# Two transformer layers on one core: features laid out so that one DMA carries a part, fp32 queries and projections in layer one, and scalings of two numbers written one number at a time

## The reference

```python
x = x + tanh(g_xattn[0]) * attention0(layernorm(x), ctx)            # w_q, w_k, w_v, w_o, no bias
x = x + tanh(g_ffn[0])   * ternary_ffn(layernorm(x))                # 256 -> 1024 -> 256, weights rounded to -1, 0, 1
x = x + tanh(g_xattn[1]) * attention1(layernorm(x), ctx, distances) # scores - log(distance) * |scale|
x = x + tanh(g_ffn[1])   * expert_ffn(layernorm(x))                 # relu, expert 0 alone, then a layernorm

def _quant_act(x):   # both inputs of the ternary FFN's matmuls
    scale = 127.0 / clip(max(abs(x), axis=-1), EPS)
    return clip(round(x * scale), -128, 127) / scale
```

## Time and profile before

| | |
|---|---|
| median of 3 runs | 430.17 us (428.62 to 430.37) |
| profiled execution | 433.62 us, span of the trace 431.9 us |
| PE busy | 333.7 us, 77% |
| DVE busy | 309.8 us, 72% |
| ACT busy | 282.7 us, 65% |
| POOL busy | 233.1 us, 54% |
| granted TensorE clock, mean | 0.920 |

### The profile page before, as it was taken

One profiled execution on the slowest core, in us unless ns is written; L12 is line 12 of the kernel. 1 busy time (PEld: TensorE's weight loads), 2 busy tenths in 40 slices (PEclk: granted clock), 3 DMA queues, 4 the chain that ended last, 5 costly groups with the idle time before them and its releaser, 6 DMA issues.

```text
span 431.9 us, 9332 instructions
## 1 busy us (share of the span) xinstructions
PE 333.7 (77%) x3346; PEld 269.8 (62%) x3346; DVE 309.8 (72%) x663; ACT 282.7 (65%) x515; POOL 233.1 (54%) x414
## 2 busy tenths in 40 slices
...
GB/s 237 278 93 180 27 62 77 29 30 30 39 40 22 0 2 1 2 0 2 8 153 128 48 50 49 49 49 44 44 11 2 2 2 27 26 26 25 26 26 49
DMA packets 34213, 21.48 MB, mean 50 GB/s; under 512 B 10359, under 2 KB 33528, under 8 KB 34091
## 3 DMA queue, kind: packets, MB, share of 16 engines
...
## 4 chain that ended last, share of the span: by engine, by line
PE 32%; DVE 26%; ACT 13%; issue 10%; POOL 7%; SPq 6%; ACTq 2%; DMA 2%; POOLq 0%; DVEq 0%
PE psA L1681 8%; PE psD L1666 4%; SPq L293 4%; PE psBE L1666 4%; DVE st L881 3%; DVE mx L1114 3%; ACT pp_hi L725 2%; DVE ham L1160 2%; POOL lns L400 2%; PE psA L1467 2%; PE psA L1448 2%; ACTq L585 2%; PE psD L1379 2%; ACT p L716 1%; DVE o L1100 1%
## 5 line engine op out<-in xcount | busy, mean ns | idle before, releaser
L498 POOL TENSOR_TENSOR pp_lo<-p,pp_hi 124x512 f16<-124x512 f32 x80 | 92.5, 1176 | 60.1 <-ACT pp_hi L725 59.9
L400 POOL TENSOR_TENSOR lns<-lns,mhalf 128x2 f32<-128x2 f32 x40 | 31.3, 782 | 114.0 <-DVE lns L886 113.7
L1114 DVE TENSOR_REDUCE mx<-psBE 128x6 f32<-128x462 f32 (+1 forms) x96 | 54.5, 579 | 31.4 <-PE psBE L1405 31.2
L716 ACT ACTIVATE p<-psD 124x512 f32<-124x512 f32 x80 | 47.7, 598 | 36.2 <-PE psD L1379 32.0
L1379 PE MATMUL psD<-qb,ktb 98*124 98x256 f16 (+1 forms) x256 | 49.4, 290 | 5.2 <-DMA qb<-mT 3.6
L725 ACT ACTIVATE pp_hi<-p 124x512 f16<-124x512 f32 x80 | 50.4, 630 | 0.0
L1379 PEld LDWEIGHTS psD<-qb,ktb 98*124 98x124 f16 (+1 forms) x256 | 34.1, 145 | 9.4 <-DMA qb<-mT 6.7
L1405 PE MATMUL psBE<-kt_hi,q_hi 128*128 128x308 f16 (+2 forms) x128 | 34.7, 313 | 4.1 <-DVE mx L1114 2.7
L1431 PE MATMUL psA<-vo,pp_hi 124*128 124x34 f16 (+1 forms) x320 | 28.0, 183 | 11.1 <-DVE xT_lo L906 4.8
L1681 PE MATMUL psA<-ew_hi,pp_lo 128*128 128x256 f16 x128 | 34.9, 273 | 0.0
L1681 PE MATMUL psA<-ew_hi,pp_hi 128*128 128x256 f16 x128 | 34.9, 273 | 0.0
...
## 6 DMA issues: line engine op xcount, KB each, us to landing
qb<-q_hi SPq DMA_DIRECT2D x128, 32.0 KB
...
```

The lines of the kernel that those rows point to most:

```text
L400: nc.gpsimd.tensor_tensor(lns[:, n % 4, 1, :], lns[:, n % 4, 0, :], mhalf[:, :], ALU.pow).then_inc(s_rs, 1)
L498: nc.gpsimd.tensor_tensor(pl[:, u % 2, 2 * r:2 * r + 2, :], p32[:, n % 4, :, :], ph[:, u % 2, 2 * r:2 * r + 2, :], ALU.subtract).then_inc( ...
L716: a_(p32[:, n % 4, :, :], psD[n % 2][0:KR, :].rearrange("p (t r) -> p t r", t=2), ACT.Exp, scale=1.0 / SSC).then_inc(a["exp"], 1)
L1114: v.tensor_reduce(mx[:, s % 2, j * H + 6 * k:j * H + 6 * k + hn], psBE[:, n % 2, 0:hn * KEYS].rearrange("p (h k) -> p h k", h=hn), AX.X, A ...
```

## The change

1. **Interleaved features.** Feature r*4+g of 128 now takes the place of feature g*32+r. Read from 128 partitions in order, the features land on 32 partitions as four runs, so each part of the queries is one DMA (`head_pairs`), 3 a unit where there were 12, and each part of the keys too. The keys' masked parts are written by DVE (`km`, four instructions), zeroed once by POOL; `keys_low` is gone, and SP issues `key_blocks` in both layers. The weights for keys and queries are copied into the new order of columns (`spread`, `spreaded`): ACT makes `wkp` and `wqp`, and the low half of layer 1's query weights takes four instructions. Masks of heads come from the unit matrix by a reduction on DVE. The maxima's middle piece takes three matmuls of 154 columns where it took two of 154 and 308, and their outputs lie in pairs.
2. **fp32 in layer 0.** `queries(0, u)` and `project(0, u)` are four fp32 matmuls of 256 columns each where they were 12 in fp16. So `xT` and `oT` are written once, as fp32, and `xT_lo` and `oT_lo` of layer 0 and the halves of its `wq` and `wo` are gone.
3. `keep_busy` is gone.
4. The scalings of two numbers (L1046, L1049, L1162, L1165, and `gsc` of two pairs, L997) are written one number at a time. `hq` of odd tiles lies in another buffer.

```diff
+QN = (16 * 5, 16 * 6)
+KW = 2 * KR
+KS = 2 * KEYS - KR
+MP = ((0, 5, 2), (5, 8, 1), (1, 4, 2))
...
+        wqp, wkp = [ew1[1][:, i, :].bitcast(F32).rearrange("p (k n) -> p k n", k=DK) for i in (0, 1)]
...
+        ktbf = ktb[:, :, :, :].rearrange("p g n w -> p (g n w)")
+        qb = sb("qb", [128, NQ, GH, DK, UR], F16)
...
+        def spread(w):
+
+            return w[:, :, :].rearrange("p k (c g r) -> p (k c) r g", c=DK, g=GH)
+
+        def spreaded(w):
+
+            return w[:, :, :].rearrange("p k (c r g) -> p (k c) r g", c=DK, g=GH)
...
+            def key_blocks(l):
+
+                sp.wait_ge(s_km, l + 1)
+                if l == 0:
+                    sp.wait_ge(s_const, C_KTB)
+                else:
+                    sp.wait_ge(A[0]["psc"], 5 * NU)
+                for p, t in ((0, 0), (1, 0), (2, 1)):
+                    sp.dma_start(ktb[p * QB:(p + 1) * QB, :, :, :], km[:, t, :, :]).then_inc(d_ktb, 16)
...
-                for g in range(GH):
-                    sp.dma_start(qb[p * QB:(p + 1) * QB, u % NQ, :, g, :],
-                                 t[g * QB:(g + 1) * QB, u % 2, :, :]).then_inc(d_q[u % NQ], 16)
+                sp.dma_start(qb[p * QB:(p + 1) * QB, u % NQ, :, :, :], t[:, u % 2, :, :]).then_inc(d_q[u % NQ], 16)
...
+            key_blocks(0)
...
-            for o, name in ((bq_c, "bq"), (bk_c, "bk"), (b1_c, "b1"), (bv_r, "bv")):
+            query_blocks(0, 0)
+            for o, name in ((bq_c, "bq"), (bk_c, "bk")):
+                sp.dma_start(o[:, :], io[name].rearrange("(g r) c -> r g c", g=GH)).then_inc(d_col, 16)
+            for o, name in ((b1_c, "b1"), (bv_r, "bv")):
                 sp.dma_start(o[:, :], io[name]).then_inc(d_col, 16)
-            query_blocks(0, 0)
...
-            def keys_low(l):
-
...
-                for r in (0, 1):
-                    i = nc.gpsimd.tensor_scalar(
-                        kml[:, :, :, r * KEYS:(r + 1) * KEYS].rearrange("p c b k -> p (c b) k"),
-                        ksp[1][:, :, :].rearrange("p c (b k) -> p (c b) k", b=B), pmask[:, r:r + 1], None, ALU.mult)
-                i.then_inc(s_ktl, 1)
...
+            nc.gpsimd.memset(km[:, :, :, :].rearrange("p a n w -> p (a n w)").bitcast(F32), 0.0)
...
+            def ln0_transposed(u):
+                act.wait_ge(L0["pxT"], u + 1)
+                a_(xTf[:, u, :, :].rearrange("p c r -> p (c r)"), (psG if u == 1 else lnb(u))[:, :],
+                   ACT.Copy).then_inc(L0["xT"], 1)
...
-            def key_blocks():
...
-                        act.dma_start(ktb[p * QB:(p + 1) * QB, :, g, at],
-                                      kt[rows, :, :, cols].rearrange("p c b k -> p (c b) k")).then_inc(d_ktb, 16)
...
+            def keys_spread(l):
+
+                act.wait_ge(d_w[l, "k"], 16)
+                ge(act, s_kp, l)
+                a_(spreaded(wkp), spread(wraw[l, "k"]), ACT.Copy).then_inc(s_wkp, 1)
...
+            keys_spread(0)
             tables_k(0)
-            weights_hi(0, "q")
-            xT_hi(L0, 0, psX)
-            xT_hi(L0, 1, psG)
+            act.wait_ge(d_w[0, "q"], 16)
+            a_(spreaded(wqp), spread(wraw[0, "q"]), ACT.Copy).then_inc(s_wqp, 1)
+            ln0_transposed(0)
+            ln0_transposed(1)
...
+                a_((oTf[:, u % 2, :, :], oTs[:, u % 2, 0, :, :])[l], psX[:, :].rearrange("p (c r) -> p c r", c=DK),
+                   ACT.Copy).then_inc(a["oTh"], 1)
...
-                v.tensor_tensor(ksp[1][:, :, :], k32[:, :, :], ksp[0][:, :, :], ALU.subtract).then_inc(s_ks, 1)
+                link(v.tensor_tensor(ksp[1][:, :, :], k32[:, :, :], ksp[0][:, :, :], ALU.subtract))
+                ge(dve, d_ktb, 3 * 16 * l)
+                for p in (0, 1):
+                    for r in (0, 1):
+                        i = v.tensor_scalar(km[:, p, :, r * KEYS:(r + 1) * KEYS],
+                                            ksp[p][:, :, :].rearrange("p c (b k) -> p (c b) k", b=B), pmask[:, r:r + 1],
+                                            None, ALU.mult)
+                i.then_inc(s_km, 1)
...
-            dve.wait_ge(s_const, C_HMASK)
-            v.tensor_reduce(pmask[:, :], hmask[:, :].rearrange("p (g r) -> p r g", r=2), AX.X, ALU.max)
+            dve.wait_ge(s_const, C_ID)
+            link(v.tensor_reduce(hmask[:, :].rearrange("p (g e) -> p g e", e=2),
+                                 id32[:, :].rearrange("p (e r g) -> p g e r", e=2, g=GH), AX.X, ALU.max))
+            link(v.tensor_reduce(pmask[:, :], hmask[:, :].rearrange("p (g r) -> p r g", r=2), AX.X, ALU.max))
             split_keys(0)
...
-                    v.tensor_scalar(gsc[:, :], gate[:, :], 1.0 / SY, None, ALU.mult)
+                    v.tensor_scalar(gsc[:, 0:1], gate[:, 0:1], 1.0 / SX, None, ALU.mult)
+                    v.tensor_scalar(gsc[:, 1:2], gate[:, 1:2], 1.0 / SY, None, ALU.mult)
...
-                link(v.tensor_scalar(am[:, 1, :], am[:, 0, :], EPS, 1.0 / 127.0, ALU.max, ALU.mult))
+                for j in (0, 1):
+                    i = v.tensor_scalar(am[:, 1, j:j + 1], am[:, 0, j:j + 1], EPS, 1.0 / 127.0, ALU.max, ALU.mult)
+                link(i)
                 ge(dve, a["q1"], u)
                 v.reciprocal(am[:, 2, :], am[:, 1, :]).then_inc(a["xn"], 1)
-                v.tensor_scalar(dq1[:, 2 * u:2 * u + 2], am[:, 1, :], ws[:, 0:1], None, ALU.mult).then_inc(a["dq"], 1)
+                for j in (0, 1):
+                    i = v.tensor_scalar(dq1[:, 2 * u + j:2 * u + j + 1], am[:, 1, j:j + 1], ws[:, 0:1], None, ALU.mult)
+                i.then_inc(a["dq"], 1)
...
+                        pairs = mx[:, s % 2, j * H:(j + 1) * H].rearrange("p (e q) -> p q e", e=2)
+                        v.tensor_reduce(pairs[:, MP[k][0]:MP[k][1]:MP[k][2], :],
+                                        psBE[:, n % 2, 0:hn * KEYS].rearrange("p (q e k) -> p q e k", e=2, k=KEYS),
                                         AX.X, ALU.max).then_inc(a["mx"], 1)
...
-                    if r == 3 and 0 <= u < NU:
+                    if r == 3 and l == 1 and 0 <= u < NU:
                         dve.wait_ge(a["oTh"], u + 1)
-                        v.tensor_tensor(oT[1][:, u % 2, :, :], psX[:, :].rearrange("p (c r) -> p c r", c=DK),
-                                        oT[0][:, u % 2, :, :], ALU.subtract).then_inc(a["oTl"], 1)
...
-                    v.tensor_scalar(dq2[:, 2 * u:2 * u + 2], g[:, 1, :], ws[:, 1:2], gate[:, 2:3], ALU.mult, ALU.mult)
+                    for j in (0, 1):
+                        n = 2 * u + j
+                        v.tensor_scalar(dq2[:, n:n + 1], g[:, 1, j:j + 1], ws[:, 1:2], gate[:, 2:3], ALU.mult, ALU.mult)
...
-                if s < 3:
-                    xT_lo(L0, 2 * s + 2, psX)
                 if s == 0:
                     tables_v(0, 0)
-                if s == 1:
-                    split_low(2, wraw[0, "o"], whl[0, "o"])
...
-            def keep_busy(n):
-
-                for _ in range(n):
-                    mm(psD2[:, 1, 0:UR], ones16[:, 0:128], ones16[:, :], start=True, stop=True)
...
-            keep_busy(10)
             ln0_transposes(0)
-            keep_busy(6)
...
-                for hf, c0, c1, o0 in (((0, 0, 6, 0),), ((0, 6, 8, 0), (1, 0, 4, 2)), ((1, 4, 8, 0),))[k]:
+                for hf, c0, c1, o0 in (((0, 0, 6, 0),), ((1, 4, 6, 0), (0, 6, 8, 2), (1, 6, 8, 4)), ((1, 0, 4, 0),))[k]:
                     i = mm(psBE[:, n % 2, o0 * KEYS:(o0 + c1 - c0) * KEYS], q[0][:, u % 2, hf, j * 128:(j + 1) * 128],
-                           kt[:, hf, b, c0 * KEYS:c1 * KEYS], start=first, stop=(k != 1 or hf == 1))
...
-                pe.wait_ge(a["oTl"], u + 1)
-                w = whl[l, "o"]
+                if l == 1:
+                    pe.wait_ge(a["oTl"], u + 1)
...
+                        if l == 0:
+                            i = mm(o, oTf[:, u % 2, c, rows_], wraw[0, "o"][:, c, :], start=first,
+                                   stop=(j == 1 and c == DK - 1))
+                            first = False
+                            continue
                         for x_, w_ in ((0, 0), (0, 1), (1, 0)):
-                            i = mm(o, oT[x_][:, u % 2, c, j * 128:(j + 1) * 128], w[w_][:, c, :], start=first,
...
-                xh, xl = parts(xT, u)
-                w = whl[l, "q"]
+                xh, xl = parts(u)
                 for c in range(DK):
                     for k in range(DK):
+                        if l == 0:
+                            i = mm(psQ[:, c * UR:(c + 1) * UR], wqp[:, k, c * 128:(c + 1) * 128], xTf[:, u, k, :],
+                                   start=(c == 0 and k == 0), stop=(c == k == DK - 1))
+                            continue
```

More of the change, by code:

```diff
@@ L102, in build @@
         whl = {}
-        for l in (0, 1):
-            for w in "qo":
-                whl[l, w] = [sb(f"w{w}{l}_{p}", [128, DK, D], F16) for p in ("hi", "lo")]
+        for w in "qo":
+            whl[1, w] = [sb(f"w{w}1_{p}", [128, DK, D], F16) for p in ("hi", "lo")]
```

(8 more changed lines are left out.)

187 lines of the change are left out of this document (72 added, 115 removed).

## The result

The changed kernel takes 416.98 us (median of 4 runs, 415.23 to 417.56), the kernel before 429.39 on the same chip: a ratio of 0.9707, interval 0.9663 to 0.9751. 417.3 was forecast. Layers are counted from 0 here, as in the program: "layer one" of the title, with the fp32 queries, is layer 0.

A forecast was written before the change was run, and what follows sets the result against it. The bound was taken to change by stage: DVE with ACT close, SP's queue in layer 1, PE from 268.8 us. Terms summed to -12.9: 420.7 profiled, 3.45 lower 417.3 as median; range 408 to 426.

The forecast's parts named there:

- A: Start to slot 1 of layer 0: later first maxima and ACT's freed time nearly meet, +0.7 us, bounds -0.3 and +1.7.
- so +2.1: Start: without keep_busy the first queries run at half clock, 3.46 us against 1.32 for twelve matmuls at full clock.
- B: Slots 1 to 3 of layer 0: xT_lo, wo_lo and gsc time removed, longer queries added, -2.7 us, bounds 0 and -7.
- Removed from the chain: xT_lo with 6.2% of 50.3 us, 3.1 us: Slots 1 to 3 of layer 0: dropping xT_lo takes its 6.2% share off the chain, 3.1 of 4.5 us removed.
- C: Slots 4 to 8 of layer 0: DVE gets 8.2 us back and ACT leads, -4.0 us, bounds 0 and -8.2.
- ACT keeps 49.8: Slots 4 to 8 of layer 0: ACT's busy time stays 49.8 us and ACT becomes the leader.
- F: Layer 1: fewer DMAs on SP end PE's waits for mT, new work lies beside other work, -5.0 us, bounds -1.6 and -6.8.
- D: 140 to 172 us: two fp32 projections alone on the path cost more, +1.3 us.
- One of each: 140 to 172 us: one projection at full clock, 0.4 us more, and one at half clock, 0.85 more, +1.3.
- E: Ternary FFN: one-number scalings shorten DVE's list until ACT leads, -3.2 us, bounds 0 and -3.8.
- with 6 of the 8 units here: Ternary FFN: 0.63 us a unit comes back for six of eight units, 3.8 us off DVE.
- slower: Rival: PE loses its full clock in slots 4 to 8 of layer 0, 16.8 us more, 434.1; chance 0.07.

The follow-up runs named there:

- matmuls on ones: The changed kernel with the 52 keep_busy matmuls before the end of slot 0 back at their old places: 415.09 us, ratio 0.959.
- singles alone: The kernel before with only the four scalings of the quantisations written one number at a time: 424.59 us against 432.97, ratio 0.981.
- pairs again: The changed kernel with the four scalings of the quantisations on two numbers at once again, gsc left as changed: 422.42 us.
- second profile: The changed kernel measured and profiled once more with no edit: 417.4 us, ratio 0.970.
- four copies: The changed kernel with every part of the queries copied in four DMAs again, 12 a unit and not 3, both layers: 422.13 us.

## Why the prediction was right

The total was right, 417.3 for 416.98, but by terms that were off both ways, and that they met is luck. The terms as measured here add up to the 16.8 us between two profiled executions, 4 more than the 12.9 forecast; the medians are 12.4 apart. Point by point:

- **A, start, +0.7.** Measured 0.0 in the first profile, 0.9 and 0.7 in the others (29.6, 30.5, 30.3 against 29.6). Right. The half-clock queries, 3.62 for 3.46, and the later maxima, 4.0 for 3.7, came as written. With the matmuls on ones back, the first queries took 1.89 us and slot 0 ended at 27.6: the 2 us are what the step "so +2.1" had put on half clock.
- **B, slots 1 to 3, -2.7.** Measured -8.8, or -6.8 against the 48.2 us of singles alone. The mechanism was right, the size not. The step that failed is "Removed from the chain: xT_lo with 6.2% of 50.3 us, 3.1 us". It priced xT_lo at its own duration. The price was its place: behind q_lo, which waits for q_hi, which waits in ACT's line, while PE waits for the bank. The subtraction alone, put back, costs 9.2 us, 4.9 of the 6.5 in its profile in these slots. The two waits in the earlier trace rows, 4.81 and 2.41, were the better row to price it by, and stood in the bounds (-7).
- **C, slots 4 to 8, -4.0.** Measured -1.1 in four of the five slots. The scalings came close to their size on DVE (16 in four slots took 2.8 us where 0.14 each gives 2.2) and are worth 2.0 in the stretch, by pairs again as by singles alone. "With ACT at 0.89 of a stretch" was nearly right; ACT went to 0.87. The step that failed is "ACT keeps 49.8": in slots 4 to 7 ACT had 41.0 us before, 40.5 in singles alone, and 42.0 now. The two copies of layer 1's weights into the new order of columns lie there, `wkp` (L583, new, 1.11 us) and `wq_hi` (L575, 1.10 for 0.63), on the engine that now leads, and the changed kernel takes 48.2 us where singles alone takes 47.2. Term F had put such work "beside other work". That these copies are the 1.0 us fits, but no run moved them.
- **D, +1.3.** From the end of slot 7 to the first ham nothing moved, 23.4 and 23.2 us. From the first to the second ham it took 11.7 us before and 13.2 now (12.9 and 13.2 in the other profiles). Each of these holds one of the "Two projections alone on the path". The step that failed is "One of each": it gives both projections the same clock before and after. The first took 2.03 us before, with the granted clock at 0.63, and takes 1.89 now, at 1.00. The second is longer, as worked out: 2.01, 1.95 and 1.74 us for 1.32. The rest of the 1.5 us is TensorE's clock again. Four matmuls just ahead of it ran at nearly full speed in the kernel before, here:

```profile
161.17 0.98 PE psBE L1600 x4
```

and at half speed in the changed kernel, as in every other one with a row in the table (1.67 to 1.71 us):

```profile
151.18 1.71 PE psBE L1600 x4
```

- **E, ternary FFN, -3.2.** Measured +0.6 (-0.5 with the second profile) between the first and the last ham, and -4.9 at the boundary, which had no term. The eight ham maxima are apart by 11.7, 9.0, 7.7, 6.9, 8.4, 8.4 and 8.4 us before, and by 13.2, 9.4, 7.5, 6.9, 8.7, 7.7 and 7.7 now. So the scalings give 0.7 in each of the last two steps, and pairs again has 8.4 there once more: the price a unit, 0.63, was right. The step that failed is "with 6 of the 8 units here": only the last two steps, and the boundary behind them, got shorter by it. What sets the steps between wasn't read. What hides the gain between first and last ham is the first step, 1.5 us longer, told under D. It isn't the products for km or the split of the query weights in four: singles alone has neither, and its first step is 13.0.
- **F, layer 1, -5.0.** Measured -2.4 in slots 1 to 3 of layer 1, and four copies put back cost 2.7 there and 3.2 at the boundary, 4.7 in all. The sum was right, and about half of it lay one slot earlier than I put it, in the copies of unit 0. The mechanism was too: PE's wait for mT in layer 1 fell from 5.2 us to 1.1, the longest 0.7 where at most 0.5 was written. What is late next is DVE's maxima, 2.2 us once.

The rule of the Trainium skill (SBUF — State Buffer, Who interferes with whom), that tensor_scalar takes the pair of ports shared with GpSimd only in its two-port form, is borne out for the four scalings: one-number ones took 0.14 to 0.27 us in the same places. The 0.26 of the one with two scalars a partition is more than the 0.14 of the earlier trace rows; its shortest pair took 0.27 as well, so it isn't a wait for POOL. The rule of the same skill that spoke against the change (TensorE: Matmul & The Clock Gate, Part 1) held at the start, though for a shorter time than A took from it: the first queries ran at 1.2 GHz, those of unit 1, at 23.44 us and still ahead of the first scores, at 2.4. With the matmuls on ones back the ratio was 0.959. In slots 4 to 7 the granted clock stayed at 0.96 (0.97 before), so the rival "slower" had no ground.

Singly undone, the parts cost 5.0 (pairs), 4.7 (copies) and 7.1 (fp16), 16.8 in all, less some 2 that ones may give: 14.8, for a whole of 12.4 to 16.9 us, depending on the chip. That agrees within this spread and proves no more; singles alone gave 8.4 and not 5.0.
